# A third block of values in f16 halves in a long-convolution decoder layer, and coarser maxima of g

## What is computed

```
def _L0_xattn_ref(k, v, q, ssm_kernel, D, head_dim):      # k = v = ctx (16, 256, 512), q = x
    k_, v_, q_ = (a.reshape(B, H, head_dim, L) for a in (k, v, q))      # H = 32, head_dim = 8, L = 512
    kv = jnp.einsum('bhil,bhjl->bijhl', k_, v_)
    y = jnp.fft.irfft(jnp.fft.rfft(kv, n=2 * L) * jnp.fft.rfft(ssm_kernel, n=2 * L), n=2 * L)[..., :L]
    out = y + kv * D[None, None, None, :, None]
    out = jnp.einsum('bijhl,bhil->bjhl', out, q_)
    ...
def _bitlinear(x, w):                                     # twice, with a GELU between
    ...
    scale = 127.0 / jnp.maximum(jnp.max(jnp.abs(x), axis=-1, keepdims=True), EPS)
    x_quant = jnp.clip(jnp.round(x * scale), -128.0, 127.0) / scale
    ...
```

## Time and profile before

| | |
|---|---|
| median of 3 runs | 997.69 us (995.42 to 998.8) |
| the profiled execution, its own time | 998.75 us |
| its span, first to last instruction | 997.0 us |
| granted TensorE clock, mean | 0.987 |
| busy: TensorE, VectorE, ScalarE, GpSimd | 94%, 82%, 63%, 54% |
| stage of the heads, to the last convolution | about 440 to 957 us |

### The profile page before, as it was taken

How to read it: one execution, slowest core, us unless ns; L and a number is a source line. 1 busy time by engine, 2 the same in 40 slices (tenths; PEclk the granted TensorE clock), 3 DMA queues, 4 the chain that set the end, 5 groups by cost and what they waited for, 6 DMA issues and landing times.

```text
span 997.0 us, 14896 instructions
## 1 busy us (share of the span) xinstructions
PE 937.2 (94%) x4490; PEld 545.7 (55%) x4490; DVE 816.0 (82%) x1650; ACT 632.5 (63%) x783; POOL 543.1 (54%) x823
## 2 busy tenths in 40 slices
PE   3989999899889999989999999999999999999985
PEld 2545544555335544445566666666666666666641
DVE  6877986399357476687999999999999999999982
ACT  4756545332356565761577777877777787777774
POOL 5302310033100000157888989889898989889851
PEclk9999999899999999999999999999999999999998
DMA  9235677456756657876386876757575665758433
GB/s 320 56 90 154 191 241 234 157 179 205 235 175 211 191 199 253 279 200 198 109 174 135 160 157 137 178 121 182 129 170 142 150 162 130 177 121 188 84 74 85
DMA packets 210268, 167.86 MB, mean 168 GB/s; under 512 B 125861, under 2 KB 166857, under 8 KB 208169
## 3 DMA queue, kind: packets, MB, share of 16 engines
q1 hardware_dynamic: 210216, 167.24, 61.9%
HBM read 112.36 MB, written 33.87 MB: 147 GB/s over the span
## 4 chain that ended last, share of the span: by engine, by line
PE 66%; DVE 14%; DMA 9%; ACT 5%; issue 4%; SPq 2%; DVEq 0%; POOL 0%; POOLq 0%; ACTq 0%
PE conv_bank L1549 17%; PE slot_bank L574 14%; PE hq_bank L1635 11%; PE conv_bank L1559 6%; PE back_bank L1656 4%; PE ff_bank L1656 4%; DMA x_scratch<-res 4%; PE slot_bank L616 4%; DVE conv_all L906 3%; PE conv_bank L595 3%; PE back_bank L1624 1%; PE back_bank L1544 1%; DMA v_ct<-v_scratch 1%; ACT conv_all L769 1%; DVE x_lo L894 1%
## 5 line engine op out<-in xcount | busy, mean ns | idle before, releaser
L906 DVE SCALAR_TENSOR_TENSOR conv_all<-u,taps,conv_all 128x1024 f32<-128x1024 f32 x92 | 122.4, 1331 | 104.2 <-ACT conv_all L769 102.4
L2002 POOL TENSOR_TENSOR sum<-z 128x512 f32<-128x512 f32 x128 | 162.9, 1273 | 23.6 <-DVE z L1865 23.6
L1635 PE MATMUL hq_bank<-x_lo,hq_t 128*128 128x512 f16 x512 | 121.9, 383 | 4.0 <-DMA hq_t<-hq_int 4.0
L616 PE MATMUL slot_bank<-wout_t,y 128*128 128x512 f32 x256 | 114.0, 600 | 3.7 <-DVE res L926 3.7
L761 ACT ACTIVATE u<-slot_bank,bias,unscale 128x1024 f32<-128x1024 f32 x46 | 55.4, 1205 | 94.5 <-PE slot_bank L574 68.7
L2006 POOL TENSOR_TENSOR sum<-sum 128x256 f32<-128x256 f32 x128 | 94.7, 740 | 10.0
L574 PE MATMUL slot_bank<-x_hi,w_hi 128*128 128x512 f16 x384 | 93.1, 385 | 7.5 <-ACT conv_all L769 5.9
L574 PE MATMUL slot_bank<-x_lo,w_hi 128*128 128x512 f16 x384 | 92.5, 383 | 3.0 <-DVE x_lo L894 3.0
L574 PE MATMUL slot_bank<-x_hi,w_lo 128*128 128x512 f16 x384 | 91.9, 382 | 0.0
L1744 ACT ACTIVATE hq_f<-g,h_scale 128x1024 f32<-128x1024 f32 x64 | 73.2, 1144 | 23.5 <-DVE h_scale L1913 19.5
L1918 DVE TENSOR_REDUCE g_max<-g 128x1 f32<-128x512 f32 x128 | 83.9, 676 | 4.8 <-ACT g L1783 4.8
(11 more groups left out here) (203 smaller groups left out, 1930.1 us busy)
## 6 DMA issues: line engine op xcount, KB each, us to landing
block_diag<-in_ctx_turned SPq DMA_DIRECT2D x32, 512.0 KB, 3.8
x_quad<-in_w_t SPq DMA_DIRECT2D x10, 1024.0 KB, 7.7
stage<-in_ctx SPq DMA_DIRECT2D x16, 512.0 KB, 6.6
v_scratch<-conv_all SPq DMA_DIRECT2D x16, 512.0 KB, 4.1
c_scratch<-v_tok SPq DMA_DIRECT2D x8, 1024.0 KB, 5.3
y<-c_scratch SPq DMA_DIRECT2D x8, 1024.0 KB, 4.9
res<-in_x SPq DMA_DIRECT2D x32, 256.0 KB, 3.2
x_scratch<-res SPq DMA_DIRECT2D x32, 256.0 KB, 3.3
```

The costliest lines, as they stand in the source:

```text
L616: last = nc.tensor.matmul(out_bank(R), y[:, cc, t, :], w["wout_t"][:, cc, :], start=(cc == 0), stop=(cc == DC - 1))
L906: ins = nc.vector.scalar_tensor_tensor(out=acc, in0=(u_first[kind] if n < 3 else u)[:, t0 + tap:t0 + tap + T // 2, :].rearrange("p t b -> ...
L1635: last = nc.tensor.matmul(hq_bank[:, :], hq_t[:, fc, :], w["w2_t"][:, fc, :], start=(fc == 0), stop=(fc == FC - 1))
L2002: nc.gpsimd.tensor_tensor(sum2[:, :, :].rearrange("p t (s j) -> p t s j", j=HD), view(z[:, b, :, :], 0, (SEGS * SEG, T), (SEG, half), (1, ...
```

## The change

Block 2 of kv is used in f16 halves too, in tb = 2 and tb = 3. For that, a fourth window of the kernel is kept in halves (HALVES = 4: window 1, lag 1, beside windows 0 and 3 and the difference), so toep_half, its load and `halve_ssm` grow; ScalarE casts blocks 0 and 2 in one instruction of 1152 elements; GpSimd still makes the rest of block 0, and VectorE makes that of block 2, in a new `split_lo` behind `measure_x2`. TensorE waits for both rests (kv_lo_done counts two per head) ahead of tb = 0. The maxima of g are taken over two pieces of 1024 columns: the first behind dn of tb = 2, waiting for the second GELU, the other behind the new subtraction, waiting for the fourth.

```diff
-HALVES = 3
+HALVES = 4
...
+            near = view(ssm_pad, P, (1, 2 * P))
+            near_hi, near_lo = view(ssm_split, 6 * P, (1, 2 * P)), view(ssm_split, SPLIT_ROW + 6 * P, (1, 2 * P))
             nc.vector.tensor_copy(wide_hi, wide)
+            nc.vector.tensor_copy(near_hi, near)
             link(nc.vector.tensor_copy(last_hi, last))
+            nc.vector.tensor_tensor(near_lo, near, near_hi, ALU.subtract)
...
-    kv_hi = sb("kv_hi", [P, 2, T, PAIRS], F16)
-    kv_lo = sb("kv_lo", [P, 2, T, PAIRS], F16)
+    kv_hi = sb("kv_hi", [P, 2, 2 * T, PAIRS], F16)
+    kv_lo = sb("kv_lo", [P, 2, 2 * T, PAIRS], F16)
...
-    g_max = sb("g_max", [P, 4 + 1])
+    g_max = sb("g_max", [P, 2 + 1])
...
-        def product_of_first(head, tb, window, start, stop, seeded=False):
+        def product_of_halves(head, tb, window, start, stop, seeded=False, block=0):
...
-                                            values[:, head.buf, hh * T // 2:(hh + 1) * T // 2, :],
+                                            values[:, head.buf, block * T + hh * T // 2:block * T + (hh + 1) * T // 2, :],
...
-                pe.wait_ge(kv_lo_done, head.count(1, 1))
+                pe.wait_ge(kv_lo_done, head.count(2, 2))
...
-                    last = product_of_first(head, tb, int(tb > 0), start=True, stop=(tb == 0))
+                    last = product_of_halves(head, tb, int(tb > 0), start=True, stop=(tb == 0))
+                elif sb_ == 2:
+                    last = product_of_halves(head, tb, 3 * (tb - sb_), start=False, stop=(sb_ == tb), block=1)
...
-            product(head, 2, 0, block(head, 2), start=False, stop=True, seeded=True).then_inc(conv_full, 1)
+            product_of_halves(head, 2, 0, start=False, stop=True, seeded=True, block=1).then_inc(conv_full, 1)
...
-            nc.scalar.copy(kv_hi[:, head.buf, :, :], kv[head.buf][:, 0:T, :]).then_inc(kv_hi_done, 1)
+            nc.scalar.copy(view(kv_hi[:, head.buf, :, :], 0, (T * PAIRS, 2), (1, T * PAIRS)),
+                           view(kv[head.buf], 0, (2 * T * PAIRS, 2), (1, T * PAIRS))).then_inc(kv_hi_done, 1)
...
+        def split_lo(head):
+
+            dve.wait_ge(kv_hi_done, head.count(1, 1))
+            if head.c >= 2:
+                dve.wait_ge(conv_full, head.back(2).count(4, 4))
+            nc.vector.tensor_tensor(kv_lo[:, head.buf, T:2 * T, :], kv[head.buf][:, 2 * T:3 * T, :], kv_hi[:, head.buf, T:2 * T, :],
+                                    ALU.subtract).then_inc(kv_lo_done, 1)
...
-            dve.wait_ge(g_maxed, head.count(4, 4))
+            dve.wait_ge(g_maxed, head.count(2, 2))
...
-            dve.wait_ge(g_done, head.count(4, k + 1))
-            nc.vector.tensor_reduce(g_max[:, k:k + 1], g[:, k * 512:(k + 1) * 512], AX_X, ALU.max,
+            dve.wait_ge(g_done, head.count(4, 2 * k + 2))
+            nc.vector.tensor_reduce(g_max[:, k:k + 1], g[:, k * 1024:(k + 1) * 1024], AX_X, ALU.max,
...
-            if h2.exists():
-                max_of_g(h2, 0)
             if n.exists():
                 times_q_dn(n, 2)
             if h2.exists():
-                max_of_g(h2, 1)
+                max_of_g(h2, 0)
             if n.exists():
                 times_q_up(n, 2)
...
+            if n.back(-1).exists():
+                split_lo(n.back(-1))
             if h2.exists():
-                max_of_g(h2, 2)
-                max_of_g(h2, 3)
+                max_of_g(h2, 1)
             if n.exists():
                 times_q_dn(n, 3)
 
         room_free(dve)
+        split_lo(Head(0))
...
-            nc.gpsimd.tensor_tensor(kv_lo[:, head.buf, :, :], kv[head.buf][:, 0:T, :], kv_hi[:, head.buf, :, :], ALU.subtract).then_inc(kv_lo_done, 1)
+            nc.gpsimd.tensor_tensor(kv_lo[:, head.buf, 0:T, :], kv[head.buf][:, 0:T, :], kv_hi[:, head.buf, 0:T, :], ALU.subtract).then_inc(kv_lo_done, 1)
```

More of the change, by code:

```diff
@@ L1608, in third_block_far @@
             else:
-                product_of_first(head, 2, HALVES - 1, start=False, stop=False, seeded=True)
+                product_of_halves(head, 2, 2, start=False, stop=False, seeded=True)
         def third_block_near(head):
@@ L2049, in gpsimd_part @@
         room_free(pool)
-        nc.gpsimd.memset(g_max[:, 4:5], EPS).then_inc(eps_made, 1)
+        nc.gpsimd.memset(g_max[:, 2:3], EPS).then_inc(eps_made, 1)
         nc.gpsimd.memset(eps_col[:, :], EPS).then_inc(eps_made, 1)
```

## The result

The changed kernel takes 1032.69 us (median of 5 runs, 1031.59 to 1038.64) where the kernel before takes 997.69: 1.0349 times as long [1.0319, 1.038]. The forecast was 1029, in a range of 1008 to 1041. So the change makes the kernel 3.5% slower, by about what was foretold. One execution of e8_two_passes (3386.97 us) and one of the kernel before beside it (3505.82 us) lie far off all others: the ratio leaves them out, the medians hold them, and without them they would be 989.51 and 998.80 instead of 989.84 and 999.06. The profiled execution is the longest of the five (1038.64, span 1036.8). The heads and the tail hold the other 36.2.

A forecast was written before the change was run, and what follows sets the result against it. VectorE and TensorE were taken as level, VectorE with 0.1 to 0.3 us of room per head. Loop 22.0, unrolled 5.7, first heads 2.2 and tail 1.1 made 31.0 us more: 1029 us, range 1008 to 1041.

The forecast's parts named there:

- What bounds the kernel: In the heads: VectorE and TensorE are level, each with only 0.1 to 0.3 us of room per head.
- The shorter products: Block 2's products on TensorE: f16 saves 0.45 us per head, worth nothing once VectorE leads.
- The subtraction: On VectorE behind measure_x2: waits 0.80 us for GpSimd at the shared port, 1.34 us to the next instruction.
- VectorE's own cycle: VectorE's time per head without waits for TensorE: 15.88 us in the loop, 15.53 unrolled, before the change's additions.
- the loop's term: The loop's 20 heads, each 15.88 + 1.22 - 16.00 us longer: 22.0 us in all.
- The unrolled heads: Six unrolled heads, each 15.53 + 1.22 - 15.80 us longer: 5.7 us in all.
- the bare price: Rival, chance 0.20: the subtraction costs only its own 0.66 us, the port being free or not needed; 1009 us.
- The dearer case: Rival, chance 0.07: the subtraction takes 1.72 us in every head beside GpSimd, net 1.60; 1040 us.
- The maxima: On VectorE: a 1024-wide maximum takes 1.13 us against 1.19 for two of 512; both merges save 0.12 per head.
- TensorE's wait for both rests: Ahead of tb = 0 in the heads: costs nothing, as shared_product waits for VectorE's z anyway.
- the first heads' term: First heads, including the start: 2.2 us more, between -1 and 4.
- The tail: Last two FFNs: the closing maximum waits for the last GELU and is 0.53 us longer; 1.1 us together.

The follow-up runs named there:

- e8_two_passes: The changed kernel with block 2's rest neither made nor multiplied, two f16 passes per product instead of three: 989.84 us, ratio 0.99.
- e2: The changed kernel without VectorE's subtraction; block 2's rest stays zero and is still multiplied: 996.42 us, ratio 0.9987.
- e5: The changed kernel with block 2's two products in f32 as before; cast, subtraction and waits stay: 1033.64 us, ratio 1.0353.
- e3: The changed kernel with the subtraction replaced by a reduction over the same 576 columns, one SBUF operand, rest left zero: 1009.79 us, ratio 1.0134.
- e9: The changed kernel with block 2's rest neither made nor multiplied, and the four 512-column maxima of before: 992.83 us, ratio 0.9948.
- e10: The changed kernel with the four 512-column maxima of the kernel before: 1035.99 us, ratio 1.0367.
- e6: The changed kernel with the subtraction moved behind times_q_dn(n, 3), TensorE waiting for it only ahead of third_block_near: 1013.61 us, ratio 1.0135.
- e7: The changed kernel with only TensorE's wait for block 2's rest moved to third_block_near, subtraction left in place: 1035.28 us, ratio 1.0367.
- e1: The kernel before with the merged 1024-column maxima alone: 1000.64 us, ratio 1.0032.

## Why the prediction was right, step by step

**What bounds the kernel: right.** VectorE had a few tenths of a us of room per head before L1877, and no more, if about twice what the list of waits gave in the loop (below). e2, e5 and e8 bear it out from three sides: take the subtraction away and the loss goes; make TensorE slower again and nothing happens; without the subtraction VectorE's cycle is what is left.

**The shorter products: right.** Worth nothing in the change (e5), as forecast. Without the subtraction the heads fall by half of the 0.45 (e2: 16.00 to 15.78, merged maxima included); that only part of the chain between the two engines runs through these products is the likely reason, argued from the waits of e2 and not tested.

**The subtraction: right in kind, and two terms were mis-sized that cancel.** It starts 4.36 us after a_mv (forecast 4.35) and ends 0.61 after GpSimd's sum for tb = 2 (forecast 0.62, the bare stream). The row of L935 in the earlier trace rows, which ended 0.28 after L2002 where L935 takes 0.52 alone, does not show that a whole stream follows; this case's runs do. That sum ends not 5.15 but 5.48 after a_mv, since I took its distance from a_mv as fixed. The a_rstd started 0.56 instead of 0.25 after a_mv: by now GpSimd's own kv_lo (to 701.78) comes last there, not a_mv. That the subtraction holds GpSimd's L2021 for 0.40 us is not the reason: in e3 and e8, where nothing holds L2021 (0.74), the sum for tb = 2 ends as late, 5.39 and 5.38 after a_mv in the mean of the loop, against 5.39 in the change and 5.16 before. So from its start to the next instruction it is 1.65 us in that head, not 1.34 (1.50 in the mean of the loop, from e8).

The other term is VectorE's own cycle: 15.88 less 0.12 was taken, and e8 measures 15.60. I had taken off the 2.4 us of waits that the rows name before L1877; e9, with before's maxima and no wait for TensorE, shows 15.74 in place of 15.88. The traces show where the rest lies. From the start of o_stats (L1931) to the start of L1877 the kernel before takes 0.85 us in the mean of the loop's 20 heads, e9 0.61 (the same two instructions in its file): 0.24 per head, 4.7 us in all, nearly the whole 0.26 from 16.00 to 15.74. The list of waits counts 10 of these heads; in the other 10 the gap is 0.06 or 0.07 us and not listed, and where VectorE doesn't wait there is no gap at all, as L1877 then starts 0.08 before o_stats ends.

15.60 + 1.50 and 15.76 + 1.34 are the same 17.10: the loop's term, 22.0 against 21.9, is as exact as that by luck, and each half of it was off by 0.16. (The two may hang together: where GpSimd's own chain fixes the end of the sum, what VectorE saves ahead of the subtraction comes back as standing still, as e10 shows for 0.06 us. The forecast did not see that, and no run tests it for the 0.16.) The unrolled heads, with 1.13 instead of 0.95 each, show the price without the luck: VectorE's cycle there is 15.33 (e8), forecast 15.41, and the subtraction adds 1.60.

The Trainium skill, "SBUF — State Buffer", section "SBUF: two separate sides", has VectorE and GpSimd take a port pair as an exclusive lock, where the loser stands for the whole instruction of the other. The runs agree: 1.73 us and an end 0.61 behind GpSimd's in the change, in e6 0.75 where L2027 stood instead (1.08 us) and 0.80 to 0.99 where L2027 had started 0.08 us or more ahead, and 0.74 in e3, where one SBUF operand beside GpSimd's L2017 was not held. An f16 operand doesn't take it out of the lock.

**The rivals**: the bare price, 1009 (its terms add up to 1009.6), is what e3 (1009.79) and e6 (1013.61) take, and so a good number for a kernel that was not the changed one. The dearer case had the size of the stall (1.72) nearly right for single heads, but not the cycle that it adds to.

**The maxima: right.** From its start to the next instruction the 1024-wide one takes 1.13 us (702.72 to 703.85), just as worked out, and the merge is worth 0.14 per head where VectorE leads (e9). Behind the meeting with GpSimd half of it is lost again (e10: 0.06).

**TensorE's wait for both rests: right in the steady heads, wrong in the first.** I priced it at nothing, as shared_product waits for z anyway; e7 shows just that. In the first of the heads listed above, to which with its neighbours and the start I gave 2.2 us (between -1 and 4; measured 5.5), it is not covered. TensorE's order there, kernel after:

```profile
485.20 0.41 PE L1563 MATMUL conv_bank<-kv_hi,block_diag 128*128 128x288 f16 x2 [2.22 <-DVE kv_lo L1848]
...
486.19 1.06 PE L616 MATMUL slot_bank<-wout_t,y 128*128 128x512 f32 x1
```

And the stretches about it, kernel after (the column behind the counts in brackets is TensorE's granted clock):

```profile
478.00:483.00 5.00, 4.99 (x27) 3.25 (x25) 4.86 (x13) 2.40 (x4) 4.68 (x7) 1.00 0.14 52
483.00:488.00 5.00, 2.80 (x9) 1.59 (x10) 4.96 (x12) 1.35 (x2) 3.93 (x6) 0.77 0.56 153
488.00:493.00 5.00, 5.00 (x16) 2.39 (x14) 1.67 (x4) 0.62 (x1) 3.47 (x6) 0.89 0.99 241
```

TensorE waits 2.22 us for the subtraction, and the granted clock of that stretch is 0.77, of the next 0.89: it is 0.50 (1.2 GHz) from 485.66 to 489.07 and 1.00 (2.4 GHz) on either side. The first of the late matmuls in it, L616, takes 1.06 us, against a mean of 0.61. With e7's later wait this head takes 19.26 us and the clock stays at 1.00 in it. Between these two executions that is 2.7 of the 3.3 us that the first heads' term lacks. But the one of the change is its slowest, with the lowest mean clock of the five (0.978 against 0.981 to 0.985), and the medians (1032.69, and 1035.28 for e7) show no gain; how much of it a usual execution loses is not shown. e5, with a wait of 1.75 us there and the clock at 1.00, takes 20.26.

A second loss was not foreseen either: in the next head the granted clock is 0.89 instead of 1.00, and so it is in e2, e7 and e8. e2, without the subtraction, takes 1.9 us more than before for these two heads (34.31 against 32.41). The merged maxima alone don't do it: e1 takes 32.41 like the kernel before, with the clock at 1.00. With the clock at 1.00 the second of these heads takes 14.06 before and 14.55 to 15.29 in e3, e5 and e10; at 0.89 or 0.90 it takes 15.74 to 16.30 (the change, e2, e6, e7, e8). So part of the loss goes with the clock; how the rest is shared between the longer cast, the maxima and the waits was not told apart, with one trace of each kernel.

**The tail**: 1.9 instead of 1.1, of which 0.5 lies in the last two heads; e1, e8 with e9, and e10 give 2.1, 1.6 and 0.6 us for the merged maxima there.

## What to carry to other kernels

Before work is moved to an engine "with room", read its room from the stage and from the waits, not from the share of the span: here VectorE's 82% was 0.3 us of room per head in the loop and 0.4 unrolled (e9: 15.74 of 16.00, 15.41 of 15.80). Take a wait from the distance between the starts of two instructions, with it and without it, and not from the list of waits alone: the list named half of the 4.7 us before L1877. Price a VectorE instruction with two SBUF operands by what GpSimd does at that moment: it ended one whole stream after GpSimd's instruction, and moving it four instructions down (with the wait for it) took some 20 us off the kernel. A distance read from the trace of before stays fixed only as long as the same wait ends last; look which engine comes last once the new work is in.

## What the hardware showed that was not expected

The lock works both ways, and the one that is held pays it inside its own duration: GpSimd's second sum took 1.14 us instead of 0.74 in the change and its third 1.08 instead of 0.45 in e6, with no wait shown; VectorE's "busy" time rose by 1.52 us per head for an instruction that takes 0.75. And in the change one wait of 2.2 us in TensorE's list was followed by a granted clock of 0.50 from 485.66 to 489.07 us, in which work that has nothing to do with the change became slower (L616, 1.06 us instead of 0.61).
